# Two wide attention sums: two of each four tiles are weighed by VectorE in one instruction, two by ScalarE

## The reference

```python
def gat_conv(x, src, dst, W, att_src, att_dst, bias, n_nodes):
    h = (x @ W).reshape(n_nodes, Hh, Cc)                      # 4 heads of 64
    a_src = (h * att_src).sum(-1)
    a_dst = (h * att_dst).sum(-1)
    alpha = leaky_relu(a_src[src] + a_dst[dst])
    m = jax.ops.segment_max(alpha, dst, num_segments=n_nodes)
    e = jnp.exp(alpha - m[dst])
    denom = jax.ops.segment_sum(e, dst, num_segments=n_nodes)
    w = e / jnp.clip(denom, 1e-16)[dst]
    out = jax.ops.segment_sum(w[:, :, None] * h[src], dst, num_segments=n_nodes)
    return out.reshape(n_nodes, Hh * Cc) + bias
```

## Time and profile before

| what | value |
|---|---|
| median of the runs | 6240.7 us (3 runs, 6237.93 to 6245.58) |
| span of the recorded execution | 7734.3 us, 106232 instructions |
| the recorded execution's own time | the page gives none beside its span |
| PE busy | 5082.7 us, 66% of the span |
| PEld busy | 3796.0 us, 49% |
| POOL busy | 3605.2 us, 47% |
| DVE busy | 3438.7 us, 44% |
| ACT busy | 2462.9 us, 32% |
| L1161, the weighing on ScalarE, both wide sums | 3360 instructions, 825.7 us, 333 ns each |

### The profile page before, as it was taken

One profiled execution on the slowest core, in us unless ns is written; L12 is line 12 of the kernel. 1 busy time (PEld: TensorE's weight loads), 2 busy tenths in 40 slices (PEclk: granted clock), 3 DMA queues, 4 the chain that ended last, 5 costly groups with the idle time before them and its releaser, 6 DMA issues. The chain is left out here.

```text
span 7734.3 us, 106232 instructions
## 1 busy us (share of the span) xinstructions
PE 5082.7 (66%) x21008; PEld 3796.0 (49%) x21009; DVE 3438.7 (44%) x11807; ACT 2462.9 (32%) x8267; POOL 3605.2 (47%) x3760
## 2 busy tenths in 40 slices
PE   3376666776777777766677766665865546445897
PEld 0143433564555555555444656665643323223676
DVE  3376667215444444454666633333344444445211
ACT  2254442115666667632444411111220001000222
POOL 4315550563555455534555255554436653654221
PEclk6687786896666766668788855555986667666899
DMA  2002221213222222223222110011223332332445
GB/s 62 3 18 79 79 80 51 69 45 99 74 76 77 75 76 78 75 87 105 82 79 79 48 12 6 6 6 16 69 88 83 84 83 58 84 82 70 149 172 176
DMA packets 298400, 549.57 MB, mean 71 GB/s; under 512 B 86168, under 2 KB 180034, under 8 KB 297922
## 3 DMA queue, kind: packets, MB, share of 16 engines
q0 software_dynamic: 165344, 389.02, 19.1%
q1 hardware_dynamic: 119852, 146.38, 5.9%
q10 hardware_dynamic: 13110, 13.08, 0.5%
HBM read 478.43 MB, written 69.80 MB: 71 GB/s over the span
## 5 line engine op out<-in xcount | busy, mean ns | idle before, releaser
L1432 PE MATMUL psM<-G,S 128*128 x3328 | 1282.6, 504 | 1058.2 <-DVE XN L1483 598.7
L1396 POOL DMA_INDIRECT G<-table_ones,ids x1176 | 1135.5, 966 | 1169.5 <-ACT ids L1365 801.2
L1432 PEld LDWEIGHTS psM<-G,S 128*128 128x128 f32 x3328 | 723.3, 245 | 1450.4 <-issue 1367.2
L1188 POOL DMA_INDIRECT G<-table_gat,ids x840 | 811.4, 966 | 657.4 <-ACT ids L1150 376.3
L1237 PE MATMUL psM<-G,S 128*128 128x260 f32 (+1 forms) x2752 | 898.4, 485 | 245.9 <-ACT G L1161 151.9
L1483 DVE TENSOR_TENSOR XN<-XN,psM 128x257 f32 (+1 forms) x1680 | 702.7, 418 | 760.0 <-issue 457.4
L1237 PEld LDWEIGHTS psM<-G,S 128*128 128x128 f32 x2752 | 705.4, 305 | 390.2 <-DVE acc L1255 170.1
L1214 PE MATMUL psE<-AD,St 128*128 x2800 | 537.4, 320 | 470.8 <-ACT St L1154 333.6
L1161 ACT ACTIVATE G<-G 128x64 f32<-128x64 f32 x3360 | 825.7, 333 | 16.2 <-issue 9.3
L1255 DVE TENSOR_TENSOR acc<-acc,psM 128x260 f32 (+1 forms) x1388 | 451.7, 325 | 806.7 <-remote 401.0
L1214 PEld LDWEIGHTS psE<-AD,St 128*128 128x128 f32 x2800 | 549.0, 284 | 532.4 <-issue 512.0
(11 more groups left out here) (465 smaller groups left out, 7545.1 us busy)
## 6 DMA issues: line engine op xcount, KB each, us to landing
w1s<-in_L_ffn_W SPq DMA_DIRECT2D x32, 1024.0 KB, 8.9
w2s<-in_L_ffn_W SPq DMA_DIRECT2D x32, 1024.0 KB
land<-out_by_choice SPq DMA_DIRECT2D x75, 256.0 KB, 3.2
G<-table_ones,ids POOLq DMA_INDIRECT x1176
G<-table_gat,ids POOLq DMA_INDIRECT x840
rows_by_token<-XN SPq DMA_DIRECT2D x20, 640.0 KB, 3.3
G<-table_ffn_gat,ids POOLq DMA_INDIRECT x548
table_ones<-XN SPq DMA_DIRECT2D x10, 640.0 KB
```

Source lines behind the costliest of these rows:

```text
L1188: pool.indirect_dma_start(G[:, g, j, :], None, table, bass.IndirectOffsetOnAxis(ids[:, g, j:j + 1], 0)).then_inc(gathered[g], 16)
L1396: pool.indirect_dma_start(G[:, k % RG * EG + j, :], None, table, bass.IndirectOffsetOnAxis(ids[:, k % GB, j:j + 1], 0)).then_inc(gathered[ ...
L1432: nc.tensor.matmul(psM[:, j, 0:W], S[:, g, j, :], G[:, bass.ds(at[g * EG + j], 1), :].rearrange("p a w -> p (a w)"), start=True, stop=True ...
```

## The change

In the wide sums `weigh_rows` handles only the first two tiles of each group (`BY_ACT` = 2), eight instructions instead of sixteen. VectorE takes the other two in one instruction over 128 partitions x 2 tiles x 4 heads x 64, where the narrow sum already had one for all its four tiles. It has a semaphore of its own, `weighed_too`, for which TensorE waits as well. In the narrow sum `BY_ACT` is 0: VectorE does all four tiles as before. The rings keep their sizes.

Apart from this, `groups_due` becomes 16 bits wide; its values are worked out through scratch space and written once, and the slots are worked out before them instead of after.

```diff
-        groups_due = {e.name: sb(f"groups_due_{e.name}", [1, e.tiles // EG], I32) for e in (LA, LB)}
+        groups_due = {e.name: sb(f"groups_due_{e.name}", [1, e.tiles // EG], U16) for e in (LA, LB)}
...
-            link(nc.vector.tensor_scalar(due[:, :], gi[:, 0, :].rearrange("p (k j) -> p k j", j=EG)[:, :, EG - 1], EG.bit_length() - 1, None, ALU.logical_shift_right))
-            link(nc.vector.tensor_scalar(due[:, :], due[:, :], float(GB + 1), None, ALU.add))
-            return nc.vector.scalar_tensor_tensor(out=slot[e.name][:, :], in0=gi[:, 1, :], scalar=float(-RING), in1=gi[:, 0, :], op0=ALU.mult, op1=ALU.add)
+            link(nc.vector.scalar_tensor_tensor(out=slot[e.name][:, :], in0=gi[:, 1, :], scalar=float(-RING), in1=gi[:, 0, :], op0=ALU.mult, op1=ALU.add))
+            last = gi[:, 0, :].rearrange("p (k j) -> p k j", j=EG)[:, :, EG - 1]
+            link(nc.vector.tensor_scalar(gi[:, 1, 0:e.tiles // EG], last, EG.bit_length() - 1, None, ALU.logical_shift_right))
+            return nc.vector.tensor_scalar(due[:, :], gi[:, 1, 0:e.tiles // EG], float(GB + 1), None, ALU.add)
...
                 on_act = c == 64
+                BY_ACT = EG // 2 if on_act else 0
...
-                            for j in range(EG):
+                            for j in range(BY_ACT):
                                 for h in range(HEADS):
...
-                                pe.wait_ge(weighed, i * GB + (g + 1))
+                                if on_act:
+                                    pe.wait_ge(weighed, i * GB + (g + 1))
+                                pe.wait_ge(weighed_too, i * GB + (g + 1))
...
                                 dve.wait_ge(powered, i * GB + (g + 1))
-                                if not on_act:
-                                    gas = G[:, g, :, HEADS * c:HEADS * c + HEADS]
-                                    gh = G[:, g, :, 0:HEADS * c].rearrange("p j (h c) -> p j h c", h=HEADS)
-                                    nc.vector.tensor_tensor(gh, gh, gas.unsqueeze(3).to_broadcast([P, EG, HEADS, c]), ALU.mult).then_inc(weighed, 1)
+                                gas = G[:, g, BY_ACT:EG, HEADS * c:HEADS * c + HEADS]
+                                gh = G[:, g, BY_ACT:EG, 0:HEADS * c].rearrange("p j (h c) -> p j h c", h=HEADS)
+                                nc.vector.tensor_tensor(gh, gh, gas.unsqueeze(3).to_broadcast([P, EG - BY_ACT, HEADS, c]), ALU.mult).then_inc(weighed_too, 1)
```

More of the change, by code:

```diff
@@ L9 @@
 U32 = mybir.dt.uint32
+U16 = mybir.dt.uint16
 ALU = mybir.AluOpType
@@ L1131, in edge_sum @@
                 summed, added, cleared = sem("summed"), sem("added"), sem("cleared")
-                turned_s, turned_c, fetched, scored, powered, weighed = (sem("turned_s"), sem("turned_c"), sem("fetched"),
-                                                                       sem("scored"), sem("powered"), sem("weighed"))
+                turned_s, turned_c, fetched, scored, powered, weighed, weighed_too = (sem("turned_s"), sem("turned_c"), sem("fetched"),
+                                                                       sem("scored"), sem("powered"), sem("weighed"), sem("weighed_too"))
                 z_step = sem("z_step")
```

## The result

The changed kernel takes 6260.38 us (median of 11 runs, 6256.76 to 6264.99), the kernel before 6245.58 us (11 runs beside them). The ratio is 1.0026, with a 95% interval from 1.0018 to 1.0034: 14.8 us slower. The forecast was 6226 us and faster; the number 6261 had been given to rival 2.

The account below looks back on a forecast made before the run. Unrecorded, GpSimd's gathers were taken to set a beat near 5.22 us a group. Terms -23 (ScalarE relieved), +12 (held gathers) and -4 (ends) gave -15 us: 6226 us from 6240.7, with an 8-in-10 range of 6185 to 6261 us.

Parts of the forecast that it names:

- rival 2: Wide sums: VectorE's weighing holds gathers back at random phases, 24 us lost, no steady gain; 6261 us, chance 0.17.
- Recording has lengthened it by 1493.6 us: Whole kernel: recorded span 7734.3 us against the unrecorded median 6240.7, about 24%, put down to recording.
- GpSimd's beat of 5.22 us: Wide sums: four gathers take GpSimd 5.22 us a group without waits; the unrecorded beat was taken to be near this.
- The gain of 0.11 us a group, 23 us: Wide sums: eight weighings leaving ScalarE gain 0.11 us in each of 208 groups, 23 us.
- the slack of 4.1 us on the path of the ids: Wide sums: ids for the gather three groups ahead are ready 4.1 us before GpSimd needs them, 6.0 after the change.
- the bound of 50 us: Wide sums: most that relieving ScalarE could gain, half of the 0.48 us a group between wide and narrow sum.
- VectorE's weighing at 0.68 us: Wide sums: the new two-tile instruction takes 0.68 us a group, at no cost under GpSimd's beat.
- Held gathers: Wide sums: gathers starting under VectorE's new instruction are held back; 12 us lost, half of the random-phase 24.
- The ends: Uncovered weighing at the end of each wide sum gets shorter: 2 x 1.92 = 4 us gained.
- The 16-bit counts: Loads of groups' due counts into TensorE's sequencer, 104 times 0.33 us: change of width taken as 0.
- Rival 1: GpSimd's beat is met in both kernels, so only the ends move: 6237 us, chance 0.27.
- The signs: Changed profile: 1680 ScalarE weighings, 208 or so VectorE ones at 0.66 to 0.70 us, wide gather mean above 966 ns under contention, clock near 0.68.

Follow-up runs that it names:

- the 16-bit kernel: The kernel before with only the 16-bit due counts and their reordered steps, all wide weighing on ScalarE; 6241.03 us, 1.0008 of the kernel before.
- dummy_psum: Kernel before with 16-bit counts plus an idle 128x512 VectorE multiplication at the new weighing's place, second input in PSUM; 6242.45 us, 1.0011 of the kernel before.
- the SBUF and PSUM pairs: VectorE's weighing, or an idle instruction in its place, with second input in SBUF against PSUM: 6260.38 against 6240.46 us, and 6255.55 against 6242.45 us.
- dummy_sbuf: Kernel before with 16-bit counts plus an idle 128x512 VectorE multiplication at the new weighing's place, both inputs in SBUF; 6255.55 us, 1.0032 of the kernel before.

## Why the prediction was wrong, point by point

- "Recording has lengthened it by 1493.6 us": wrong. The changed kernel is recorded in 6256.6 us and runs in 6260.4. The gap was between the two kinds of chip. From it I took rightly that the median's runs have a beat near that of the gathers, and wrongly that their waits can be read from this trace.
- GpSimd's beat of 5.22 us: mis-sized. The two wide stages of the 16-bit kernel take 534 us for 105 groups with the 6.5 us of one long gather each, which leaves 5.02 us a group. The 5.22 had a boundary of 1.46 us between two groups; undisturbed, it is 1.25 as inside a group.
- The gain of 0.11 us a group, 23 us: this is the step that failed. It was the middle between nothing and a bound that I drew from the narrow and the wide sum of one trace, and that trace was of a chip on which the paths through ScalarE are long. With GpSimd's idle time 266.2 us before and 266.0 after it is zero. The difference that the bound came from is nearly gone too: on the chips of the median the narrow sum takes 690 / 137 = 5.04 us a group and the wide one 534 / 105 = 5.09, 0.05 apart and not 0.48. The narrow sum of the 16-bit kernel, beside its wide ones above:

```profile
3480.00:4170.00 690.00, 599.35 (x2746) 577.94 (x2746) 295.85 (x1642) 130.53 (x410) 520.76 (x548) 0.50 0.17 8
```

  I had the reason in the text, the slack of 4.1 us on the path of the ids, and did not let it decide: no row showed the slack running out on a chip of the median. On the chips of the trace's kind the bound of 50 us was too low in two of three cases: the change with the moved bias gains 43, 55 and 103 us by its ratios.
- VectorE's weighing at 0.68 us, and free in its own queue: right, 686 ns, and dummy_psum shows it free.
- Held gathers, 12 us between 0 and 24: the mechanism right, the size 14.9 us in busy time (824.6 - 809.7), 0.07 us a group. That the middle between fixed and random phases came so near is luck in part, for neither holds. The phases are fixed and harmless for most groups: in the first sum 13 of 104 weighings hold a gather. In the second sum 48 do, and 45 of these are the first or second weighing of a trip of four: the two changed stages took 538 and 545 us, against 534 and 534. What the second sum has more is the bias addition at the start of a trip; that it puts the next two weighings onto a gather is read from the timeline and was not tested on these chips. The first group of a trip in the changed kernel, the bias addition, the weighing and the gather that starts with 0.23 us of it left (the gather under the second group's weighing is of the kind shown above, with 0.41 us left):

```profile
2072.48 0.42 DVE L2031 TENSOR_TENSOR X<-X,row_gat 128x256 f32 x1 [1.25 <-issue]
2072.82 0.69 DVE L1292 TENSOR_TENSOR G<-G 128x512 f32<-128x512 f32 x1
...
2073.28 1.04 POOL L1191 DMA_INDIRECT G<-table_gat,ids  x1 [0.30 <-issue]
```

- The rule of the Trainium skill (SBUF — State Buffer, Who interferes with whom) that such an instruction contends with GpSimd's reads is borne out by the SBUF and PSUM pairs. That the loser blocks for the whole instruction is not quite: the gather loses 0.13 us less than the remainder, and an instruction that starts after the gather has begun holds nothing (175 cases). The same section's inference that descriptor generation is not stopped by it is contradicted by the 14 us of dummy_sbuf.
- The ends, 4 us: zero where it can be seen. From the last gather of the first wide sum to the first gather of the second it is 50.0 us in the changed kernel (1945.56 to 1995.52) and 50.0 in the 16-bit kernel (1940.96 to 1990.94).
- The 16-bit counts, 0: 1.0008 with 1.0 inside the interval. The other kernels here with these counts and no gather held by a weighing are at 1.0006, 1.0006 and 1.0011, on the same side, so a cost of some 4 us is possible and not shown.
- Rival 1 was right in that GpSimd's beat is met in both kernels and nothing is gained; it left out the held gathers. Rival 2 had the right sign and mechanism. Its 6261 us came from 24 us at random phases less 4; the runs gave 15 and no 4, so that it meets the measured 6260.4 us by luck.
- The signs: 1680 weighings on ScalarE, VectorE's at 686 ns, and the mean of a wide gather at 982 ns came as they should. The granted clock is 0.84 and 0.83 in the wide stages instead of 0.68, but it is 0.83 in the 16-bit kernel too: it differs between the kinds of chip and not by the change.

## What to carry to other kernels

First ask of a recorded execution whether it stands for the runs: a span 24% above the median may be from other conditions than the runs, and a gain must be read where the median lives, in the idle time of the engine that sets the beat. A relieved engine gives nothing while that idle time is at its floor, and an instruction is not free because its engine has room: here its second input in SBUF was charged to GpSimd. Moving that one input to PSUM took the charge away at equal work.

## What the runs showed of the hardware that I had not expected

- Some chips ran the same kernel in 6233 to 6246 us and others in 7570 to 7723 us, and the best division of work between ScalarE and VectorE is opposite on them: 1.0163 against 0.9882 for the same kernel.
- A gather is held only if the VectorE instruction with two SBUF inputs is already running when it starts, by what is left less 0.13 us (0.41 left, 0.28 longer; 0.86 left, 0.73 longer; 62 gathers of one trace).
- Twice as long an instruction (128x1024 for 128x512) cost 94 instead of 15 us of gather time.
